# Adding scatters into two tables by token, and statistics and norm read from PSUM, in an attention and mixture-of-experts kernel

## What the kernel computes

```python
w, idx = _gate(xf, wg)                    # 4 experts of 32 a token, and their weights
pos = (jnp.cumsum(oh, axis=0) * oh).sum(-1) - 1
keep = pos < cap                          # cap = 640 rows an expert
...
buf_tok = jnp.full((E * cap + 1,), N, jnp.int32).at[dest].set(tok)[:-1]
...
h = jax.nn.silu(jnp.einsum('ecd,edh->ech', xe, w1)) * jnp.einsum('ecd,edh->ech', xe, w3)
out = jnp.einsum('ech,ehd->ecd', h, w2) * buf_w.reshape(E, cap, 1)
y = jnp.zeros((N + 1, DIM), x.dtype).at[buf_tok].add(out.reshape(E * cap, DIM))[:N]
z = jax.nn.silu(xf @ sw1) * (xf @ sw3) @ sw2
...
x = _layernorm(x + y + z)
```

## Time and profile before

| | |
|---|---|
| three runs, us | 963.58, 967.00, 969.57 (median 967.0) |
| the profiled execution, us | 966.79 |
| its span, us | 965.0 |
| mean granted TensorE clock | 0.943 |
| TensorE busy | 827.7 us (86%) |
| GpSimd busy | 693.3 us (72%) |
| VectorE busy | 619.7 us (64%) |
| ScalarE busy | 610.4 us (63%) |

### The profile page before, as it was taken

How to read it: one execution, slowest core, us unless ns; L and a number is a source line. 1 busy time by engine, 2 the same in 40 slices (tenths; PEclk the granted TensorE clock), 3 DMA queues, 4 the chain that set the end, 5 groups by cost and what they waited for, 6 DMA issues and landing times.

```text
span 965.0 us, 24771 instructions
## 1 busy us (share of the span) xinstructions
PE 827.7 (86%) x8909; PEld 631.5 (65%) x8909; DVE 619.7 (64%) x2350; ACT 610.4 (63%) x1174; POOL 693.3 (72%) x626
## 2 busy tenths in 40 slices
PE   4789999989999999999999999896689776778725
PEld 1357787767877777778777777775357554556412
DVE  4777777967888897797797798583543222222107
ACT  3278887878788887887889789774314333332205
POOL 7046656568878868868969868877637777777756
PEclk9699999999999999999999999998699999998858
DMA  6686677744434433534444434203224444443247
GB/s 173 180 270 201 204 205 212 190 108 110 121 76 130 117 95 102 137 82 122 114 96 120 109 89 104 61 22 111 88 92 129 118 125 132 127 120 116 63 177 279
DMA packets 100618, 126.14 MB, mean 131 GB/s; under 512 B 18739, under 2 KB 61194, under 8 KB 99600
## 3 DMA queue, kind: packets, MB, share of 16 engines
q1 hardware_dynamic: 91280, 107.70, 40.2%
q0 software_dynamic: 9216, 16.86, 5.6%
HBM read 33.96 MB, written 42.24 MB: 79 GB/s over the span
## 4 chain that ended last, share of the span: by engine, by line
PE 68%; DMA 9%; DVE 7%; issue 5%; POOL 4%; ACT 3%; SPq 3%; ACTq 0%; DVEq 0%; POOLq 0%
PE PS L1012 7%; PE PS L1037 6%; PE PS L1061 6%; PE PS L1064 6%; PE PS L1212 6%; PE PS L1026 4%; DMA Q<-xe_rows 4%; PE PS L1081 4%; PE PS L1083 3%; PE PS L1082 3%; DMA y_rows<-BIG,Q 3%; PE PS L1110 3%; POOL y_rows L1886 3%; PE PS L1111 3%; PE PS L1090 3%
## 5 line engine op out<-in xcount | busy, mean ns | idle before, releaser
L1844 POOL TENSOR_TENSOR PL<-PF,PH 128x1280 f16<-128x1280 f32 x128 | 336.3, 2627 | 70.7 <-ACT PH L1321 62.2
L1498 DVE CUSTOM_DVE_ANT_0 JUNK<-PS,M 128x512 f16<-128x512 f32 (+3 forms) x512 | 234.7, 486 | 66.2 <-PE PS L1037 62.0
L1315 ACT ACTIVATE PF<-PS 128x512 f32<-128x512 f32 (+1 forms) x384 | 193.9, 525 | 64.0 <-PE PS L1064 63.5
L1886 POOL DMA_INDIRECT y_rows<-BIG,Q x160 | 155.7, 973 | 65.2 <-issue 38.7
L1321 ACT ACTIVATE PH<-PF 128x1280 f16<-128x1280 f32 x128 | 162.5, 1270 | 2.1
L1061 PE MATMUL PS<-Q,K 128*128 128x512 f16 (+3 forms) x512 | 154.1, 301 | 5.8 <-DMA Q<-MROW 3.8
L1877 POOL DMA_INDIRECT xe_rows<-PAY,DEST x128 | 128.0, 1000 | 40.1 <-issue 27.8
L1064 PE MATMUL PS<-Q,K 128*128 128x512 f16 (+3 forms) x512 | 147.5, 301 | 0.0
L1081 PE MATMUL PS<-VH,PH 128*128 128x65 f16 x1280 | 133.6, 195 | 8.5 <-issue 5.5
L1082 PE MATMUL PS<-VL,PH 128*128 128x64 f16 x1280 | 133.7, 193 | 0.0
L1083 PE MATMUL PS<-VH,PL 128*128 128x65 f16 x1280 | 133.6, 194 | 0.0
(11 more groups left out here) (221 smaller groups left out, 1878.9 us busy)
## 6 DMA issues: line engine op xcount, KB each, us to landing
K<-KH SPq DMA_DIRECT2D x128, 128.0 KB, 2.3
Q<-QH SPq DMA_DIRECT2D x128, 128.0 KB, 2.6
xe_rows<-PAY SPq DMA_DIRECT2D x20, 520.0 KB, 3.6
Q<-xe_rows SPq DMA_DIRECT2D x32, 325.0 KB, 2.9
K<-KL SPq DMA_DIRECT2D x64, 128.0 KB, 2.3
Q<-QL SPq DMA_DIRECT2D x64, 128.0 KB, 2.5
y_rows<-PAY SPq DMA_DIRECT2D x16, 512.0 KB, 3.9
K<-in_L_ffn_w_dram SPq DMA_DIRECT2D x96, 64.0 KB
```

What stands on the lines that cost most here:

```text
L1315: e.activation(PF[:, n % PBUF, c0:c0 + width], PS[:, k, 0:width], ACT.Exp).then_inc(s["c_exp"], 1)
L1498: e.tensor_tensor_reduce(JUNK[:, n_ttr % 2, 0:width], PS[:, 2 + k, c0:c0 + width], M0[:, 512 - width:512], 1.0, -3e38, ALU.add, ALU.max, M ...
L1844: e.tensor_tensor(PL[:, n % PBUF, :], PF[:, n % PBUF, :], PH[:, n % PBUF, :], ALU.subtract).then_inc(s["c_lp"], 1)
L1886: e.indirect_dma_start(out=y4[:, :], out_offset=bass.IndirectOffsetOnAxis(ap=XE[:, x_ % 6, k, 128:129].bitcast(I32), axis=0), in_=OUT[:, x ...
```

## The change

`y_rows` goes. In its place stand two tables of sums, `y_sums0` and `y_sums1`, with one row for each token and 1024 rows more. Experts with an even number scatter into the first, those with an odd number into the second, and the DMA adds its row to what the table holds (`compute_op=ALU.add`). The row number that travels with a token is now the token's. A token comes up at most once within an expert; two experts of the same table are kept apart by a wait: before the scatters of expert x GpSimd waits until those of x - 2 have landed. Empty slots add into the 1024 rows behind the tokens. The tables must start at zero: ten fills for them in place of 16.

In the last stage two loads a part bring the two rows of a token, table 0 from SyncE and table 1 from ScalarE. TensorE adds both to X1 in PSUM, but in parts 1, 3 and 5 (`paired`) GpSimd adds them first and TensorE adds the one result. Statistics and norm read PSUM. `begin` waits for the scatters of expert 30 as well, and for the norm that frees its bank.

```diff
-    for i in range((E * CAP + N * TOPK) // FR):
+    for i in range((E * CAP + 2 * (N + FR)) // FR):
         at(F0 + int(F1 * i), fill_rows, i)
...
-    y4 = nc.dram_tensor("y_rows", (N * TOPK, C), F32, kind="Internal").ap()
+    tables = [nc.dram_tensor(f"y_sums{i}", (N + FR, C), F32, kind="Internal").ap() for i in range(2)]
...
+    paired = (1, 3, 5)
...   TensorE
-            w.wait_ge(s_acc, 2 * (i - 8) + 1)
+            w.wait_ge(s_ys[(E - 2) % 4], 80 * (E // 4))
+            w.wait_ge(s_x2, i - 7)
             e.matmul(PS[:, i % 8, 0:128 * (q1 - q0)], IDF[:, :],
                      X1[:, 4 * b + q0:4 * b + q1, :].rearrange("p q c -> p (q c)"), start=True, stop=False)
...
+            if i in paired:
+                w.wait_ge(s_pair, paired.index(i) + 1)
+                e.matmul(part, IDF[:, :], PR[:, i % 3, 0:128 * (q1 - q0)], start=False, stop=True).then_inc(s_xy, 1)
+            else:
+                w.wait_ge(l_y0[i], 16)
+                e.matmul(part, IDF[:, :], BUF[b][:, 0, f], start=False, stop=False)
+                w.wait_ge(l_y1[i], 16)
+                e.matmul(part, IDF[:, :], BUF[b][:, 1, f], start=False, stop=True).then_inc(s_xy, 1)
...   ScalarE
+        for i, (b, q0, q1) in enumerate(parts):
+            for k in range(4):
+                w.wait_ge(s_ys[k], 80 * 8)
+            w.wait_ge(*at("z", NB - 1))
+            f = slice(128 * q0, 128 * q1)
+            e.dma_start(BUF[b][:, 1, f], table_b[1][b][:, f]).then_inc(l_y1[i], 16)
...
-                r = e.activation(result_of(i)[:, q, :], sums_of(i, 0)[:, q, :], ACT.Identity,
+                r = e.activation(result_of(i)[:, q, :], sums_of(i, q1 - q0)[:, q, :], ACT.Identity,
...   VectorE
-                w.wait_ge(s_pair, i + 1)
                 w.wait_ge(s_x2, i - 2)
-                e.tensor_tensor(sums_of(i, 0)[:, 0:n, :], PS[:, i % 8, 0:128 * n].rearrange("p (q c) -> p q c", c=128),
-                                PR[:, i % 3, 0:n, :], ALU.add).then_inc(s_acc, 1)
...
-                    r = e.bn_stats(st[:, q, :], sums_of(i, 0)[:, q, :])
+                    r = e.bn_stats(st[:, q, :], sums_of(i, n)[:, q, :])
...   GpSimd
+                w.wait_ge(s_pay0, 1)
+                e.iota(pay_rows[:, 0:FR // 128, 128:129].bitcast(I32), pattern=[[1, FR // 128], [0, 1]], base=N,
+                       channel_multiplier=FR // 128).then_inc(s_fill, 1)
...
+            if x_ > 1:
+                w.wait_ge(s_ys[(x_ - 2) % 4], 80 * ((x_ - 2) // 4 + 1))
...
-                    out=y4[:, :], out_offset=bass.IndirectOffsetOnAxis(ap=XE[:, x_ % 6, k, 128:129].bitcast(I32), axis=0),
-                    in_=OUT[:, x_ % 4, k, :], in_offset=None, bounds_check=last_y4,
-                    oob_is_err=False).then_inc(s_ys[x_ % 4], 16)
+                    out=tables[x_ % 2][:, :], out_offset=bass.IndirectOffsetOnAxis(ap=XE[:, x_ % 6, k, 128:129].bitcast(I32), axis=0),
+                    in_=OUT[:, x_ % 4, k, :], in_offset=None, bounds_check=last_row,
+                    oob_is_err=True, compute_op=ALU.add).then_inc(s_ys[x_ % 4], 16)
...
-            e.tensor_tensor(PR[:, i % 3, 0:q1 - q0, :], y_of(b)[:, q0:q1, 2, :], y_of(b)[:, q0:q1, 3, :],
-                            ALU.add).then_inc(s_pair, 1)
+            if i in paired:
...
+                w.wait_ge(s_xy, i - 2)
+                e.tensor_tensor(PR[:, i % 3, :], BUF[b][:, 0, :], BUF[b][:, 1, :], ALU.add).then_inc(s_pair, 1)
             if i:
                 weigh(i - 1)
...   SyncE
-            e.dma_start(BUF[b][:, f], y4_b[b][:, f]).then_inc(l_y4[i], 16)
+            f = slice(128 * q0, 128 * q1)
+            e.dma_start(BUF[b][:, 0, f], table_b[0][b][:, f]).then_inc(l_y0[i], 16)
```

More of the change, by code:

```diff
@@ L843, in program @@
     l_w, l_xe = [sem(f"l_w{i}") for i in range(4)], [sem(f"l_xe{i}") for i in range(6)]
-    l_xa, l_y4 = [sem(f"l_xa{i}") for i in range(NB)], [sem(f"l_y4{i}") for i in range(NB + 1)]
+    l_xa = [sem(f"l_xa{i}") for i in range(NB)]
+    l_y0, l_y1 = [sem(f"l_y0{i}") for i in range(NB + 1)], [sem(f"l_y1{i}") for i in range(NB + 1)]
     s_ys, s_out = [sem(f"s_ys{i}") for i in range(4)], [sem(f"s_out{i}") for i in range(NB + 1)]
@@ L907, in five @@
         return PS[:, bank, k * 128:(k + 1) * 128] if k < 3 else PS[:, bank + 1, (k - 3) * 128:(k - 2) * 128]
-    BUF = [t[:, h:h + 2048] for t in (X1TA, ph2, HZ, ph1) for h in (0, 2048)]
-    ACC = PF[:, :, 0:1024].rearrange("p s (a n) -> p s a n", a=2)
-    y4_b = y4.rearrange("(b p f) c -> b p (f c)", b=NB, p=128)
+    BUF = [t[:, h:h + 1024].rearrange("p (t f) -> p t f", t=2) for t in (X1TA, HZ) for h in range(0, 4096, 1024)]
+    table_b = [t[0:N, :].rearrange("(b p q) c -> b p (q c)", b=NB, p=128) for t in tables]
     out_b = out.rearrange("b (q p) c -> b p q c", p=128)
@@ L922, in result_of @@
         return t[:, 512 * k:512 * k + 512].rearrange("p (q c) -> p q c", q=4)
-    PR = flat32(PL, 1536).rearrange("p (s q c) -> p s q c", s=3, q=4)
+    PR = flat32(PL, 1536).rearrange("p (s f) -> p s f", s=3)
     def stats(k3):
@@ L929, in stats, with sums_of @@
                 t[:, 32:36], t[:, 36:40], t[:, 40:44])
-    def sums_of(b, i):
-        return ACC[:, b % 3, i, :].rearrange("p (q c) -> p q c", q=4)
-    def y_of(b):
-        return BUF[b].rearrange("p (q k c) -> p q k c", q=4, k=4)
+    def sums_of(i, n):
+        return PS[:, i % 8, 0:128 * n].rearrange("p (q c) -> p q c", c=128)
+    paired = (1, 3, 5)
     parts = [(b, 0, 4) for b in range(NB - 1)] + [(NB - 1, 0, 2), (NB - 1, 2, 4)]
@@ L1246, in tensor @@
         for i, (b, q0, q1) in enumerate(parts):
-            part = PS[:, i % 8, 0:128 * (q1 - q0)].rearrange("p (q c) -> p q c", c=128)
-            w.wait_ge(l_y4[i], 16)
-            e.matmul(part, IDF[:, :], y_of(b)[:, q0:q1, 0, :], start=False, stop=False)
-            e.matmul(part, IDF[:, :], y_of(b)[:, q0:q1, 1, :], start=False, stop=True).then_inc(s_xy, 1)
+            part = PS[:, i % 8, 0:128 * (q1 - q0)]
+            f = slice(128 * q0, 128 * q1)
[7 more added lines that the diff above has]
+                e.matmul(part, IDF[:, :], BUF[b][:, 1, f], start=False, stop=True).then_inc(s_xy, 1)
             if i == 3:
@@ L1428, in vector @@
                 e.memset(PAY[:, :, :, :], 0.0).then_inc(s_pay0, 1)
-                w.wait_ge(s_pay0, 1)
-                e.memset(pay_rows[:, :, 128:129].bitcast(I32), FAR).then_inc(s_fill, 1)
                 e.memset(VH[:, :, :, :, 64:65].rearrange("p a b c d -> p (a b c) d"), 1.0)
@@ L1783, in gpsimd @@
         w = Line(e)
-        last_xe, last_y4 = e.to_reg(E * CAP - 1), e.to_reg(N * TOPK - 1)
+        last_xe, last_row = e.to_reg(E * CAP - 1), e.to_reg(N + FR - 1)
         def weigh(i):
@@ L1866, in gpsimd @@
                 for q in (2 * half, 2 * half + 1):
-                    i = e.iota(PAY[:, q, :, 128:129].bitcast(I32), pattern=[[1, 4], [0, 1]], base=b * 2048 + 4 * q,
-                               channel_multiplier=16)
+                    i = e.iota(PAY[:, q, :, 128:129].bitcast(I32), pattern=[[0, 4], [0, 1]], base=b * 512 + q,
+                               channel_multiplier=4)
                 i.then_inc(s["c_pg"], 1)
@@ L1946, in sync @@
                 else:
-                    e.dma_start(y4[j * FR:(j + 1) * FR, :].rearrange("(p k) r -> p k r", p=128),
+                    t, j = divmod(j, (N + FR) // FR)
+                    e.dma_start(tables[t][j * FR:(j + 1) * FR, :].rearrange("(p k) r -> p k r", p=128),
                                 pay_rows[:, 0:FR // 128, 0:128]).then_inc(s["c_fill"], 16)
@@ L2006, in sync @@
                 w.wait_ge(s_ys[k], 80 * 8)
-            w.wait_ge(s_oc, 5 * E)
             w.wait_ge(*at("z", NB - 1))
-            f = slice(512 * q0, 512 * q1)
-            e.dma_start(BUF[b][:, f], y4_b[b][:, f]).then_inc(l_y4[i], 16)
+            f = slice(128 * q0, 128 * q1)
+            e.dma_start(BUF[b][:, 0, f], table_b[0][b][:, f]).then_inc(l_y0[i], 16)
         for i, (b, q0, q1) in enumerate(parts):
```

9 lines of the change are left out of this document (4 added, 5 removed).

## The result

The changed kernel takes 1046.0 us (median of three, 1045.7 to 1047.6) against 965.3 us for the kernel before (median of four, 962.2 to 969.6): ratio 1.084, interval 1.078 to 1.090. It is slower by 8.4%, and the forecast of 959 us, 953 to 980, was wrong. A fourth execution took 4611 us; its cause is open, and it is left out. The profiled execution took 1045.72 us, with a span of 1044.0.

A forecast was written before the change was run, and what follows sets the result against it. Bound: TensorE in attention, GpSimd's scatters (1.278 us a step) in the expert stage, then the last stage's chain. 966.8 - 3.8 (fills) + 0.5 (landing) - 4.6 (last stage) = 958.9 us, bounds 954 to 964, range 953 to 980 (0.80).

The forecast's parts named there:

- (a) of the scatters: Expert stage, GpSimd: an adding scatter's instruction takes 0.974 us like a plain one, so 0 us.
- the right rival: Expert stage: the adding scatter instruction gets longer, up to twice 0.974 us (1114 us); chance 0.14 beyond 0.11 us, 0.08 below.
- (b) The wait for x - 2: Expert stage, GpSimd: landing within 2.2 to 5.1 us is covered by six steps, 7.67 us, so 0.
- (c) Empty slots: Expert stage: empty slots now write rows beyond the tokens; some 100 GB/s more DMA at most, covered.
- Fills, -3.8 us: Attention, around 190 us: earlier last fill removes TensorE's stall, 2.9 us plus half of 1.7 for low clock; bounds 2.0 to 4.6.
- Landing, +0.5 us: After the last expert scatter: its uncovered landing takes between 0 and 2.9 us longer, taken as +0.5.
- Last stage, -4.6 us: After the last scatter: smaller loads, warm TensorE and shorter VectorE parts end the last norm at 956.3 instead of 960.9.
- the loads find the engine at the high clock: Last stage, TensorE: X1 matmuls end at 933.6, loads land at 934.1, so a matmul of 512 takes 0.86 us, not 1.71.
- PSUM statistics: Last stage, VectorE: four statistics read from PSUM instead of SBUF cost 0 to +0.26 us, taken as +0.07.
- the waits of VectorE for GpSimd's pair adds: Last stage: GpSimd's queue delays sums, part 3 by 1.7 us, part 4 by 0.5, part 5 by 1.3.
- the landing did not outgrow its cover: Expert stage rival: landings above 7.67 us delay each pair of experts, 15 times; 994 us at 10 us; chance 0.06.
- the tail did gain: Last stage rival claimed no gain: TensorE at the low clock, last norm near 960.9, 963.5 us in all; chance 0.12.

The follow-up runs named there:

- e2: Changed kernel with eight scatter forms by expert number modulo 8 (adding or plain, 128 or 64 rows, flag, half rows): at 128 rows 1552 ns adding, 972 plain.
- e3: Changed kernel with all experts adding into table 0, each waiting for the scatters of the expert before it: 1140.6 us.
- e1: Changed kernel with its 160 scatters overwriting instead of adding: 1025.7 us beside 1031.3 for the kernel before, ratio 0.995.
- e4: Kernel before with all 36 fills kept but due six head slots earlier: 1019.1 us beside 1022.0, ratio 0.9935.
- e5: Kernel before with the X1 matmuls of the last stage waiting for expert 30's scatters, fills as before: 1021.1 us beside 1022.0, ratio 0.998.
- e7: Changed kernel with scatters overwriting instead of adding, a repeat of e1: 1028.4 us beside 1030.2 for the kernel before, ratio 0.994.
- e12: Changed kernel, adding scatters kept, with four X1 matmuls done once more: 1076.9 us beside 1031.9 for the kernel before, single execution.
- e11: Kernel before with GpSimd waiting once an expert for all five of ScalarE's copies instead of once a scatter: 1039.1 us beside 1031.9, ratio 1.006.

## Why the prediction was wrong

**The step that failed** is (a) of the scatters: "I take 0.974, since the two rows there differ in row size and in index source and still agree within 2%. 0 us". The price of the adding instruction was put at that of a plain one; it measured 1.542 us. 159 steps longer by 0.568 are 90.3 us, and the stage grew by 88.9; of the 1.93 us of idle time in the earlier trace rows, 1.6 more than the usual 0.30, nothing is left. The agreement of two rows was weak evidence: both belong to plain scatters of 128 rows, so they tell that row size and index source cost little (e2 confirms it for row size), and nothing of a kind of operation that neither of them does. The prediction had the right place, the right multiplier and the right rival, and gave that rival 0.14; its formula, 958.9 + 160 times the excess, gives 1049.8 with the measured 0.568 us, 4.1 more than the 1045.7 of the profiled execution. The stretch before the first scatter gave 2.0 us more than forecast and the scatters cost 2.0 less than the formula has; that the last stage's 1.3 too little and the 1.3 behind the last norm cancel is luck. For an operation that no row shows, on an engine without slack and multiplied by 160, the lower end of the bounds was taken, with nothing in the rows to carry it.

The rule of the Trainium skill, "Collectives: The Full Stack", section on why ReduceScatter is half of AllGather, that an add in the DMA path takes two read descriptors where a copy takes one, pointed the right way; the page gives no time for the instruction. Here the instruction became 1.59 times as long, 1.48 times in its fixed part and 2.4 times in the part by rows; how many descriptors it writes, no run shows.

**(b) The wait for x - 2** costs nothing here, as predicted: a landing of 3.3 us (2.2 to 5.1 predicted) under six steps, which are 11.1 us now. e3 shows what it would cost uncovered, and e1 that the wait itself costs 0.48 us where GpSimd is not the bound. **(c) Empty slots** cost nothing visible: the DMA share is 0.57 in the stage, and the step is even. That they cost nothing is read from e1, whose instruction is as short as in the kernel that skips them.

**Fills, -3.8 us:** the stall and the low clock went as told, and e4, which moves only the fills, shows the mechanism. Measured across the place it is 4.8 us in the profiled pair and 4.3 in the pair e5 and e4, at the upper bound of 4.6 rather than in the middle, as if the low clock, counted at half in the sum, had come whole. The 5.8 us of the table hold other things as well.

**Landing, +0.5 us:** 3.19 us after the last scatter's start instead of 2.2, so +1.0, within the bounds of 0 to 2.9; 0.5 us too little in the sum.

**Last stage, -4.6 us,** with the landing -4.1 to the end of the last norm; measured -2.8. Here the failed step is "the loads find the engine at the high clock": they find it at the lower, 3.94 us after its last matmul. The prediction left a gap of 0.5 us (933.6 to 934.1). Three things made it 3.9: the X1 matmuls start 5.65 us ahead of the last scatter instead of 4.2, since five steps are longer now (1.45); they take 8.60 us instead of 9.66 (1.06); and the first table rows are there 6.89 us after the last scatter's start instead of 6.0 (0.9). With plain scatters, for which the sum was made, the stretch is 27.8 and 28.3 us in e1 and e7, against 956.3 - 928.1 = 28.2 predicted. The changed kernel's 30.0 are 2.2 more than e1's: 1.1 because its first rows are there later (6.89 us after the last scatter's start instead of 5.79), and 1.1 from then on, where its first sums run at the lower clock. The loads took 3.52 us (3.65 predicted), PSUM statistics 0.01 us more (0.07), and the waits of VectorE for GpSimd's pair adds were where they had been computed: before part 3 and part 5 1.13 us each (1.7 and 1.3 predicted) and before part 4 0.58 (0.5). Another 1.3 us came off behind the last norm, though both kernels' last store lands in 1.8 us. It goes with the add: from there to the end of the span it takes 2.8 us in the three kernels that add only (the changed one, e3, e12) and 4.1 to 4.2 in all that only write. Why is open.

Of the other rivals, the landing did not outgrow its cover, and the tail did gain, though less than forecast.

## What to carry to other kernels

An operation that the trace has never done has no price in it, however well its neighbours agree; if it goes 160 times on the engine that sets the pace, measure one of it first. A scatter's cost to GpSimd is mostly per instruction (852 of 972 ns), so fewer and fuller instructions pay and shorter rows don't; most of what an add costs, 412 of 580 ns, goes there too. When a stage upstream of a carefully timed start gets slower, time the start anew: TensorE stood still for 3.94 us behind the X1 matmuls instead of 0.5, and 1.45 of that came from the longer step alone. And measure a gain across the place where it arises: read at the first scatter, 500 us later, the fills seem to be worth 5.8 us or 3.5, and across the stall 4.8 and 4.3.

## What had not been expected of the hardware

An adding indirect scatter of 128 rows holds GpSimd 1.54 us, a plain one 0.97; by the two lines of e2, 1.26 and 0.85 us of that don't depend on the number of rows, and halving the row length changes nothing. It lands 3.3 us after its start instead of 2.2. The page's row of GpSimd's queue has 27136 packets in the changed kernel and 9216 in e1, which differs only in the add, with the same 18.98 MB in both; that is 112 packets more for each of the 160 scatters. Of the changed kernel:

```profile
q0 software_dynamic: 27136, 18.98, 14.2%
```

The 0.30 us between two scatters remain without a wait on a semaphore (e11), while behind the added wait for x - 2 a scatter that GpSimd stood ready for starts 0.48 us later (e1). And where TensorE stops for no reason that the profile shows, an 8.4% loss became 4.4% (e12, one execution), because GpSimd's longer instructions hid the stops.
